# The reads of the mixture's gates, moved behind the first two ring steps of the next forward part

## The chip, the core and the metric

The kernel runs on one core of a Trainium2 chip. Its engines are TensorE (PE; PEld is its weight load), VectorE (DVE), ScalarE (ACT), GpSimd (POOL) and SyncE (SP). SP does no arithmetic here: it issues nearly all DMAs, in the order in which they are written. The metric is the device time of one execution in microseconds (us); lower is better.

## The reference

The input is a batch of 32 images. A tower of two layers turns each into 38 tokens of 192 features:

```
h = patches @ W + positions, behind two class tokens           # 32 x 38 x 192
h = h + state_space(layernorm(h))                              # 16 states per feature, a scan over 38 steps
h = h + two_of_eight_experts(layernorm(h))                     # 192 -> 768 -> 192 with gelu
h = h + up(ln(mamba_f(down)) + flip(ln(mamba_b(flip(down)))))  # a scan forward and one backward, 16 states
h = h + mixture(layernorm(h)): softmax over 8 scores, the best 2, each a 192 x 192 matrix
```

The last two lines matter here. Both scans compute, at each step t, `state = decay[t] * state + in[t]` for 192 features x 16 states. The mixture multiplies each token by the gates of its two chosen experts (the other six gates are zero) and puts the products through the eight matrices.

## The kernel before

**Groups and passes.** The batch is cut into 4 groups of 8 images (T = 304 tokens). A first pass does the first scan and the routing of all groups, then come the experts, whose last blocks overlap the start of the second pass. The second pass does the last two lines of the reference. It handles each group g in a forward part (`part_a`) and a backward part (`part_b`), of 12 ring steps each (`QSTEPS`). Software pipelining adds other groups' work: during group g's parts, the same engines do the output and gates of group g - 1 (`tail`), the front of group g + 1 (`nxt`) and, in the forward part, the mixture of group g - 2 (`mix`). So a mixture stands in the forward parts of groups 2 and 3, and two more behind the last scan.

**A ring step.** The scan runs over 16 states x 8 features on 128 partitions, two blocks of features at a time (128 x 608). Its inputs are rows of 304 values of step size and input, which DVE computes and SP writes to DRAM (`write_rows`: six DMAs, L621 to L623) and reads back, each row broadcast to 16 partitions (`fill_slot`, L510: one DMA of 304 KB into the ring `dA` and one into `BB`). `rows_there` makes SP wait until the six writes have landed. A ring of 4 slots holds the steps; `read_rows` waits until the scan four steps earlier has been done. Then for step c:
- ACT takes the exponential of `dA` in place (L956, two instructions). By its program it works two steps ahead of the others.
- DVE multiplies `BB` into PSUM (L1293) and scans (L1304) into one of two buffers `ST`.
- POOL multiplies the state by C into `PR` (L790). A scan waits for the product two steps before it.
- PE sums the product over states with four matmuls (`sum_step`).

**The gates of the mixture.** When group g - 1's gates are ready at the end of a backward part, SP writes them to DRAM (`write_gates`, L637), writes the next group's rows, and reads the gates back, broadcast over partitions, into the buffer `GX` (in the trace: `WX`): `read_gates`, one DMA of 1216 KB (L642) and two of 304 KB (L646). In the forward part that follows, POOL multiplies `GX` by the normalized tokens in six pieces, one behind each of the products 0 to 5 (`gate_inputs`, L798). Each piece waits for all three reads (`gates_in`). PE puts each piece through the experts' matrices (`mixture`, four matmuls a piece), at ring steps 1 to 6, behind `sum_step` 0 to 5. DVE adds the result at ring step 7 (`add_mixture`, L1549), and only then computes the rows of the backward part (`steps`, L1355 to L1364), for which SP waits.

**The order of the other engines around it.** On ACT, behind the exponential of step 4 come the square and copy of the other direction's output (L985, L986), a silu for the backward direction with a table load before and behind it (L909 to L917, L839), the exponentials of steps 5 to 7, and a copy of 24 rows (L921). PE's matmuls of the backward direction's step sizes (`project_steps`, `PS<-aP`) wait for L921. They stand in PE's order ahead of the last two pieces of the mixture. All orders are written out by hand in the functions; no scheduler changes them.

Of the kernel before, what the change touches and what calls it, by code (L numbers as in the profile page):

```python
# [7 lines left out]
GROUPS = 4  # L8
# [108 lines left out]
def vit_tower(nc, x_p, c128a, c64a, c128, c64, ex_m, ex_r, ex_b, out_m, out_r):  # L117
    fp32, bf16, i32, u32 = mybir.dt.float32, mybir.dt.bfloat16, mybir.dt.int32, mybir.dt.uint32
    ALU, ACT, AX = mybir.AluOpType, mybir.ActivationFunctionType, mybir.AxisListType
    with ExitStack() as ctx:  # L120
# [353 lines left out]
        def is_first(g):  # L474
            return isinstance(g, int) and g == 0
# [5 lines left out]
        def _(sp):  # L481
# [21 lines left out]
            def fill_slot(k, c, slot, signal):  # L503

                for kind, ring in enumerate((dAq, BBq)):
                    rows, per, j = rows_d[k, kind, 0:DM, :], MAIN_BLOCKS, c * QB
                    if j >= MAIN_BLOCKS:
                        rows, per, j = rows_d[k, kind, DM:D, :], REST_BLOCKS, j - MAIN_BLOCKS
                    rows = rows.rearrange("(i j) t -> i j t", j=per)[:, j:j + QB, :].rearrange("i j t -> i (j t)")
                    sp.dma_start(ring[:, slot].rearrange("p b t -> p (b t)"),  # L510
                                 rows.unsqueeze(0).broadcast_to([NS, FB, QB * T])).then_inc(signal.sem, 16)
# [90 lines left out]
            def load_next(g):  # L602
                sp.wait_ge(mixed.sem, mixed.after(g, TILES))
                load_keep(g + 1)
                sp.wait_ge(M.residual.sem, M.residual.after(g, 1))
                load_h(g + 1)

            def store(g):
                sp.wait_ge(final.sem, final.after(g, 1))
                sp.dma_start(out_m[bass.ds(g, 1), :, :].rearrange("g p t -> p (g t)"), Om[:, :]).then_inc(stored.sem, 16)  # L610
                sp.dma_start(out_r[bass.ds(g, 1), :, :].rearrange("g p t -> p (g t)"), Or[:, :]).then_inc(stored.sem, 16)

            def store_end(g):
                sp.wait_ge(stored.sem, stored.after(g, 32))
                sp.sem_inc(out_free.sem, 1)

            def write_rows(g, k):

                sp.wait_ge(Q.w_ready.sem, Q.w_ready.after(g, k + 1))
                for kind, x in enumerate((DIRS[k].DL, DIRS[k].WV)):  # L620
                    sp.dma_start(rows_d[k, kind, 0:DM, :], x[:, 0:T]).then_inc(rows_written.sem, 16)  # L621
                    sp.dma_start(rows_d[k, kind, DM:D, 0:HALF], x[0:DR, T:PK]).then_inc(rows_written.sem, 16)
                    sp.dma_start(rows_d[k, kind, DM:D, HALF:T], x[DR:128, T:PK]).then_inc(rows_written.sem, 16)  # L623

            def rows_there(g, k):
                sp.wait_ge(rows_written.sem, rows_written.after(g, 96 * (k + 1)))

            def read_rows(g, k, c):

                n, slot = k * QSTEPS + c, c % SLOTS  # L630
                if n >= SLOTS or not is_first(g):
                    sp.wait_ge(q_scanned.sem, q_scanned.after(g, n - SLOTS + 1))
                fill_slot(k, c, slot, landed[slot])

            def write_gates(g):
                sp.wait_ge(Q.gates_T_ready.sem, Q.gates_T_ready.after(g, 1))
                sp.dma_start(gates_d[:, :], Q.LW).then_inc(gates_out.sem, 16)  # L637

            def read_gates(g):

                sp.wait_ge(gates_out.sem, gates_out.after(g, 16))
                sp.dma_start(GX[:, 0:EXPERTS, :].rearrange("p e t -> p (e t)"),  # L642
                             gates_d.rearrange("e t -> (e t)").unsqueeze(0).broadcast_to([128, EXPERTS * T])).then_inc(gates_in.sem, 16)
                for h in range(2):
                    every = gates_d.rearrange("(e h) t -> h e t", h=2)[h:h + 1, :, :]
                    sp.dma_start(GX[h * DR:(h + 1) * DR, EXPERTS:, :], every.broadcast_to([DR, EXPERTS // 2, T])).then_inc(gates_in.sem, 16)  # L646
# [12 lines left out]
            for g in range(GROUPS):  # L659
                rows_there(g, 0)  # L660
                for c in range(QSTEPS):
                    read_rows(g, 0, c)
                write_rows(g, 1)
                rows_there(g, 1)
                for c in range(QSTEPS):
                    read_rows(g, 1, c)
                    if c == 4 and g + 2 < GROUPS:
                        load_next(g + 1)
                    if c == 8 and g >= 2:
                        store(g - 2)  # L670
                    if c == QSTEPS - 1 and g >= 2:
                        store_end(g - 2)
                if g:
                    write_gates(g - 1)
                if g + 1 < GROUPS:
                    write_rows(g + 1, 0)
                if g:
                    read_gates(g - 1)
            store(GROUPS - 2)
            store_end(GROUPS - 2)  # L680
            write_gates(GROUPS - 1)
# [1636 lines left out]
```

## Time and profile before

| what | us |
|---|---|
| timed runs | 966.21, 966.85, 961.38; median 966.21 |
| the profiled execution, its own time | 961.01 |
| its span, first to last instruction | 959.2 |
| PE busy | 741.7 (77%) |
| DVE busy | 564.3 (59%) |
| ACT busy | 403.8 (42%) |
| POOL busy | 395.1 (41%) |
| forward part of group 2, from the first scan's input to `add_mixture` | 716.5 to 742.4 |
| forward part of group 3, the same | 812.7 to 838.2 |

No engine is busy throughout: the kernel is a chain of stages in which the engines wait for one another, so the busy shares do not say which one a stage waits for.
### The profile page before, as it was taken

The page shows a single profiled execution, that of the slowest core. Times are in us where ns is not written, and L with a number is a line of the kernel's source. Part 1 is how long each engine was busy: PE and PEld are TensorE (multiplying, and loading weights), DVE is VectorE, ACT ScalarE, POOL GpSimd, SP SyncE. Part 2 cuts the span into 40 slices and gives each one's busy share as a digit, 9 for nine tenths or more (in the row PEclk, how much of TensorE's full clock was granted, in tenths as well). Part 3 has the DMA queues.
Part 4 walks back from the last instruction along what each step waited for, and adds up shares of the span by engine and source line. Part 5 has one row for each costly group of instructions (what it writes and reads, how often), then busy time and mean ns, then how long its engine had stood idle before and what let it go on. Part 6 is the DMA issues. An engine that isn't in the chain of part 4 may idle for free. (4 is left out here: it accounts for less than half of the span.)

```text
span 959.2 us, 11504 instructions
## 1 busy us (share of the span) xinstructions
PE 741.7 (77%) x3608; PEld 587.3 (61%) x3608; DVE 564.3 (59%) x968; ACT 403.8 (42%) x876; POOL 395.1 (41%) x311
## 2 busy tenths in 40 slices
PE   7877887784647879887999568797769986986756
PEld 5645656553437879787899346565556764663534
DVE  4167779679675613312112587888877787789320
ACT  1548374282225224322345356373617352733110
POOL 1045745665663321321003244653538333834503
PEclk8899999797667989999999789988978999897978
DMA  9469655355585567877676778697688657967211
GB/s 349 134 211 337 206 158 143 100 148 145 144 232 150 164 193 237 262 234 232 212 232 191 196 195 223 173 239 182 153 220 218 153 141 222 240 151 191 79 61 37
DMA packets 84668, 179.51 MB, mean 187 GB/s; under 512 B 12740, under 2 KB 32832, under 8 KB 83840
## 3 DMA queue, kind: packets, MB, share of 16 engines
q1 hardware_dynamic: 79776, 171.55, 63.3%
q0 software_dynamic: 4832, 7.24, 2.6%
q8 instruction: 28, 0.46, 0.2%
q14 instruction: 32, 0.26, 0.1%
HBM read 158.02 MB, written 20.69 MB: 186 GB/s over the span
## 5 line engine op out<-in xcount | busy, mean ns | idle before, releaser
L1670 PE MATMUL PS<-PR,CM 128*128 128x304 f32 (+1 forms) x672 | 186.3, 419 | 92.7 <-POOL PR L790 63.8
L790 POOL TENSOR_TENSOR PR<-ST,V 128x608 f32<-128x608 f32 x96 | 142.3, 1482 | 185.7 <-DVE ST L1304 155.5
L1670 PEld LDWEIGHTS PS<-PR,CM 128*128 128x128 f32 x672 | 126.5, 220 | 135.7 <-POOL PR L790 77.7
L956 ACT ACTIVATE dA<-dA,negA 128x304 f32<-128x304 f32 x192 | 93.6, 538 | 151.8 <-DMA BB<-rows_d 151.7
L1304 DVE TENSOR_TENSOR_SCAN ST<-dA,PS 128x608 f32<-128x608 f32 x96 | 136.3, 1420 | 15.1 <-ACT dA L956 10.9
L1008 ACT ACTIVATE HID<-PS,WX 128x128 f32<-128x128 f32 x204 | 59.5, 367 | 149.7 <-PE PS L1670 147.6
L703 POOL TENSOR_TENSOR dA<-dA,aP 128x607 f32<-128x607 f32 x48 | 70.7, 1475 | 73.1 <-ACT aP L976 71.2
L1293 DVE TENSOR_TENSOR PS<-BB,PS 128x608 f32<-128x608 f32 x96 | 76.2, 794 | 22.5 <-DMA BB<-rows_d 11.3
L1500 DVE TENSOR_TENSOR xp<-PS,WXB 128x192 f32<-128x192 f32 x34 | 12.2, 358 | 128.2 <-PE PS L1670 123.4
L1670 PE MATMUL PS<-XT,WX 128*128 128x128 f32 x408 | 84.1, 290 | 1.0 <-ACT HID L1008 1.0
L1670 PE MATMUL PS<-XT,WXR 128*128 128x128 f32 x408 | 83.8, 289 | 0.0
L718 POOL DMA_DIRECT2D outs_d<-xp x34 | 19.4, 570 | 148.0 <-DVE xp L1500 148.0
L1670 PE MATMUL PS<-WX,HID 128*128 128x192 f32 x408 | 74.1, 331 | 7.3 <-DVE XT L1493 6.1
L1670 PEld LDWEIGHTS PS<-WX,HID 128*128 128x128 f32 x408 | 67.5, 194 | 8.2 <-issue 6.1
L709 POOL TENSOR_TENSOR PR<-PR,ST 128x608 f32<-128x608 f32 x32 | 47.2, 1474 | 57.9 <-DVE ST L1283 57.7
L1283 DVE TENSOR_TENSOR_SCAN ST<-dA,PS 128x608 f32<-128x608 f32 x48 | 67.8, 1412 | 2.3 <-issue 1.3
L1670 PEld LDWEIGHTS PS<-XT,WX 128*128 128x128 f32 x408 | 67.0, 206 | 1.3 <-ACT HID L1008 1.3
L1670 PEld LDWEIGHTS PS<-XT,WXR 128*128 128x128 f32 x408 | 66.8, 206 | 0.0
L1670 PE MATMUL PS<-WX,CM 128*128 128x304 f32 x192 | 55.6, 431 | 11.0 <-POOL WX L798 10.6
L1670 PEld LDWEIGHTS PS<-WX,CM 128*128 128x128 f32 x192 | 37.1, 197 | 26.2 <-POOL WX L798 13.6
L1670 PE MATMUL PS<-HB,CM 96*128 96x152 f32 (+1 forms) x240 | 48.5, 353 | 0.2 <-ACT HB L1110 0.2
L1670 PEld LDWEIGHTS PS<-HB,CM 96*128 96x128 f32 x240 | 39.7, 202 | 8.0 <-issue 2.7
(363 smaller groups left out, 1287.8 us busy)
## 6 DMA issues: line engine op xcount, KB each, us to landing
dA<-rows_d SPq DMA_DIRECT2D x144, 304.0 KB
BB<-rows_d SPq DMA_DIRECT2D x144, 304.0 KB
WX<-ex_m SPq DMA_DIRECT2D x34, 576.0 KB
WX<-ex_m SPq DMA_DIRECT2D x34, 387.0 KB, 3.8
slots_d<-WXR SPq DMA_DIRECT2D x8, 960.0 KB, 8.2
WXR<-ex_r SPq DMA_DIRECT2D x34, 192.0 KB, 4.6
WX<-gates_d SPq DMA_DIRECT2D x4, 1216.0 KB, 6.3
CM<-c SPq DMA_DIRECT2D x1, 4430.0 KB, 19.6
```

What stands on the lines that cost most here:

```text
L703: nc.gpsimd.tensor_tensor(now[:, 1:], now[:, 1:], before[:, 0:QB * T - 1], ALU.mult).then_inc(ap_ready.sem, 1)
L709: nc.gpsimd.tensor_tensor(PR3[c % 3], PR3[c % 3], STq[:, c % 2], ALU.mult).then_inc(P.product.sem, 1)
L718: pool.dma_start(outs_d[b // HALF_BLOCKS][at:at + 128, :], YB[:, b % 3, :]).then_inc(out_rows[b % 3], 16)
L790: nc.gpsimd.tensor_tensor(PRq[:, c % 2], STq[:, c % 2], DIRS[k].Cw.unsqueeze(1).broadcast_to([128, QB, T]), ALU.mult).then_inc(q_product.s ...
L956: last = nc.scalar.activation(dAq[:, slot, i, :], dAq[:, slot, i, :], ACT.Exp, scale=negA[:, j:j + 1])
L1008: last = nc.scalar.activation(HX[:, p, f, :], PS[:, wide_bank(b, h), j * 128:(j + 1) * 128], ACT.Gelu, bias=WX[:, p, FFN + f:FFN + f + 1])
L1283: nc.vector.tensor_tensor_scan(flat(STq[:, c % 2], False), flat(dAq[:, slot], False), BP[0], 0.0, ALU.mult, ALU.add).then_inc(P.scanned.se ...
L1293: nc.vector.tensor_tensor(BPq[k], BBq[:, slot], BW[k].unsqueeze(1).broadcast_to([128, QB, T]), ALU.mult).then_inc(b_times_w.sem, 1)
L1304: nc.vector.tensor_tensor_scan(flat(STq[:, c % 2], back), flat(dAq[:, slot], back), BP[k][:, ::-1] if back else BP[k], 0.0, ALU.mult, ALU. ...
L1500: nc.vector.tensor_tensor(YB[:, p, :], PS[:, SHARED_BANK, 256:256 + D], WXB[:, p, :], ALU.add).then_inc(y_copied.sem, 1)
L1670: return nc.tensor.matmul(out, lhsT, rhs, start=first, stop=last)
```

## The change

`read_gates` of group g - 1 stood behind `write_rows` of group g + 1 and ahead of that group's `rows_there` and ring reads. Now it stands behind ring steps 0 and 1 of the forward part of group g + 1, and ahead of ring step 2. This concerns the gates of groups 0 and 1, read in the forward parts of groups 2 and 3. The gates of groups 2 and 3 are read behind the last scan, as before. Nothing is added or removed.

```
@@ second pass, SP @@
                 rows_there(g, 0)
                 for c in range(QSTEPS):
                     read_rows(g, 0, c)
+                    if c == 1 and g >= 2:
+                        read_gates(g - 2)
                 write_rows(g, 1)
...
                 if g + 1 < GROUPS:
                     write_rows(g + 1, 0)
-                if g:
-                    read_gates(g - 1)
+            read_gates(GROUPS - 2)
             store(GROUPS - 2)
```

Only SP's order changes. On SP at the start of group 2's forward part (`q_WV` is the last of the rows written, `dA` and `BB` are the ring, `WX` takes the gates; in brackets the semaphores that an instruction waits for), - is before and + is now:

```order
 L623 DMA rows_d<-q_WV 64x152
+L510 DMA dA<-rows_d 128x1x608 [waits q_scanned,rows_written]
+L510 DMA BB<-rows_d 128x1x608
+L510 DMA dA<-rows_d 128x1x608 [waits q_scanned]
+L510 DMA BB<-rows_d 128x1x608
 L642 DMA WX<-gates_d 128x2432 [waits gates_out]
 L646 DMA WX<-gates_d 64x4x304 x2
-L510 DMA dA<-rows_d 128x1x608 [waits q_scanned,rows_written]
-L510 DMA BB<-rows_d 128x1x608
-L510 DMA dA<-rows_d 128x1x608 [waits q_scanned]
-L510 DMA BB<-rows_d 128x1x608
```

The four ring reads of steps 0 and 1 have moved ahead of the three gate reads, and the wait for the written rows with them; the reads of step 2 follow the gates. The same piece stands once more, at the start of group 3's forward part.

On POOL, at the same place, the order is the same before and now (L790 are the products of steps 0 to 2, L798 the first pieces of the gates; the line numbers are those of before):

```order
L790 TENSOR_TENSOR PR<-ST,V 128x608 [waits q_summed,c_copied,q_scanned]
L798 TENSOR_TENSOR WX<-WX,q_Xm 128x608 [waits x_doubled,gates_in]
L790 TENSOR_TENSOR PR<-ST,V 128x608 [waits q_summed,q_scanned]
L798 TENSOR_TENSOR WX<-WX,q_Xm 128x608 [waits x_doubled,gates_in]
L790 TENSOR_TENSOR PR<-ST,V 128x608 [waits q_summed,q_scanned]
```

Nothing has moved here; the first L798 waits for `gates_in`, and the product of step 1 is queued behind it.

## Rows read from the trace of the kernel before

**Rows 1.** Chain of waits by time, groups 2 and 3: start us, us, engine
```profile
711.49 7.52 issue
...
720.58 21.35 PE PS L1670 x74
...
816.74 20.92 PE PS L1670 x74
```
**Rows 2.** Timeline of SP: start us, us, engine line op out<-in
```profile
701.45 0.60 SPq L623 DMA_DIRECT2D rows_d<-q_WV  x1
702.09 0.58 SPq L642 DMA_DIRECT2D WX<-gates_d  x1
704.23 0.73 SPq L510 DMA_DIRECT2D dA<-rows_d  x1
708.54 0.52 SPq L510 DMA_DIRECT2D dA<-rows_d  x1
...
800.49 0.60 SPq L623 DMA_DIRECT2D rows_d<-q_WV  x1
801.13 0.58 SPq L642 DMA_DIRECT2D WX<-gates_d  x1
```
**Rows 3.** Timeline of DVE; in brackets the idle time before and what ended it
```profile
716.53 0.80 DVE L1293 TENSOR_TENSOR PS<-BB,PS 128x608 f32<-128x608 f32 x1 [5.67 <-DMA BB<-rows_d]
741.95 0.47 DVE L1549 TENSOR_TENSOR Om<-q_Hm,PS 128x304 f32<-128x304 f32 x1 [2.27 <-PE PS L1670]
...
812.70 0.80 DVE L1293 TENSOR_TENSOR PS<-BB,PS 128x608 f32<-128x608 f32 x1 [5.60 <-DMA BB<-rows_d]
837.68 0.47 DVE L1549 TENSOR_TENSOR Om<-q_Hm,PS 128x304 f32<-128x304 f32 x1 [2.78 <-PE PS L1670]
```
**Rows 4.** Chain of waits by time, parts without gates: start us, us, engine
```profile
844.02 1.94 DMA rows_d<-p_WV
...
846.58 4.23 DMA BB<-rows_d
```
**Rows 5.** Busy us in stretches: PE, PEld, DVE, ACT, POOL, then PEclk, DMA share, GB/s
```profile
702.00:704.00 2.00, 2.00 (x14) 1.78 (x13) 2.00 (x3) 0.00 (x0) 1.11 (x2) 1.00 0.63 127
...
720.00:722.00 2.00, 1.42 (x3) 1.09 (x4) 1.98 (x3) 0.59 (x2) 2.00 (x3) 0.50 0.97 257
...
726.00:728.00 2.00, 2.00 (x9) 1.29 (x8) 1.86 (x3) 1.78 (x5) 1.69 (x2) 1.00 0.97 248
```
**Rows 6.** Timeline of ACT, groups 2 and 3
```profile
718.94 0.99 ACT L956 ACTIVATE dA<-dA,negA 128x304 f32<-128x304 f32 x2 [1.48 <-DMA BB<-rows_d]
...
726.20 0.99 ACT L956 ACTIVATE dA<-dA,negA 128x304 f32<-128x304 f32 x2 [1.40 <-DMA BB<-rows_d]
...
730.62 0.39 ACT L917 ACTIVATE p_Xm<-PS,CM 64x152 f32<-64x152 f32 x1
...
735.99 0.40 ACT L921 ACTIVATE aP<-PS 24x304 f32<-24x304 f32 x1
...
814.84 0.99 ACT L956 ACTIVATE dA<-dA,negA 128x304 f32<-128x304 f32 x2 [1.21 <-DMA BB<-rows_d]
...
831.20 0.40 ACT L921 ACTIVATE aP<-PS 24x304 f32<-24x304 f32 x1
```
**Rows 7.** Timeline of PE, groups 2 and 3
```profile
720.58 2.40 PE L1670 MATMUL PS<-PR,CM 128*128 128x304 f32 x4 [4.86 <-POOL PR L790]
...
725.74 1.19 PE L1670 MATMUL PS<-WX,CM 128*128 128x304 f32 x4
...
732.54 0.68 PE L1670 MATMUL PS<-p_UP,CM 128*128 128x304 f32 x2
...
737.65 1.19 PE L1670 MATMUL PS<-aP,CM 128*128 128x304 f32 x6
...
833.38 1.19 PE L1670 MATMUL PS<-aP,CM 128*128 128x304 f32 x6
```
**Rows 8.** Timeline of POOL, group 2
```profile
720.47 1.48 POOL L798 TENSOR_TENSOR WX<-WX,q_Xm 128x608 f32<-128x608 f32 x1
```

More of the change, by code:

```diff
@@ L662, in _ @@
                     read_rows(g, 0, c)
+                    if c == 1 and g >= 2:
+                        read_gates(g - 2)
                 write_rows(g, 1)
@@ L676, in _ @@
                     write_rows(g + 1, 0)
-                if g:
-                    read_gates(g - 1)
+            read_gates(GROUPS - 2)
             store(GROUPS - 2)
```

## The prediction

> **What bounds the kernel now.** I read the page, then the chain of waits, then the rows of each engine in the two stretches that the edit touches. These are the starts of the forward parts of groups 2 and 3, near 711 and 806 us. The chain [rows 1] shows 7.52 us of "issue" at 711.49, a wait whose cause it doesn't see, and then 74 matmuls in one unbroken run of 21.35 us (20.92 in group 3). DVE's rows say what the hole is: it stood idle for 5.67 us until step 0's BB had landed (716.53), and for 5.60 us in group 3 (812.70) [rows 3]. SP's rows say why: behind the last write of rows (701.45) it issued the gates (702.09), and the first ring read only at 704.23 [rows 2]. In a part without gates, step 0 landed at 846.58 + 4.23 = 850.81, 4.85 us behind the landing of the rows at 845.96 [rows 4].
>
> That invites the reading that two holes of 5.6 us go. I don't read it so. In the first stretch the DMA engines don't stop at step 0. ACT waits for every BB, to step 4 at 726.20 [rows 6], and the DMA share is 0.97 at 720 and at 726 [rows 5]. This transfer-bound stretch lasts from the gates to step 4, and the edit leaves its bytes the same and permutes them.
>
> **The change, part by part.**
>
> *The start of the transfers.* Before, the gates were issued at 702.09, while SP would have had to wait for the rows anyway. Now ring step 0 is first, and it needs the rows: 1.94 us from the last write's issue to its landing [rows 4], so 701.45 + 1.94 = 703.39. Everything then starts 703.39 - 702.09 = 1.30 us later. In group 3 it is 800.49 + 1.94 - 801.13 = 1.30 again [rows 2]. The DMA share at 702 to 704 was 0.63 [rows 5]: this is the stretch that the old order filled.
>
> *Steps 0 and 1* land early: step 0 at 703.39 + 4.85 = 708.2, before DVE is free at 716.53 - 5.67 = 710.86 [rows 3]. In group 3 it is 802.43 + 4.85 = 807.3 against 807.10. Both holes vanish from where they were.
>
> *The gates.* Gates, step 0 and step 1 are the same bytes in another order, so the last of the three lands where step 1 did, plus 1.30: 718.94 + 1.30 = 720.24, and 814.84 + 1.30 = 816.14 [rows 6]. POOL's first piece of the gates, which started at 720.47 [rows 8], can start at 720.24. POOL waits for it between the products of steps 0 and 1, and DVE's scan of step 3 waits for product 1. The stall has only moved from step 0 to step 2, which stands behind the gates in the queue.
>
> *Steps 2 to 4* land 1.30 later than before, step 4 at 727.50. The three issues of the gates end at about 703.39 + 2.5 + 2.1 = 708.0, ahead of step 2's 708.54 [rows 2], so SP delays none.
>
> *From step 4 to the mixture.* ACT worked without a hole from step 4's exponential (726.20) to L921, which ended at 735.99 + 0.40 = 736.39 [rows 6]. This 10.2 us follows step 4's landing, and now ends at 737.69. PE's matmuls on that copy started at 737.65 [rows 7]: PE came 1.26 us after ACT, because its run had begun late, at 720.58. Now PE is early and waits for ACT. Its first piece of the mixture can start at 720.24 + 1.48 = 721.72 instead of 725.74, and 6.80 us of work bring it to the backward projections, which need L917: 730.62 + 0.39 + 1.30 = 732.31. From there it takes 737.65 - 732.54 = 5.11 to 737.42, still ahead of 737.69. So these matmuls start at 737.69 instead of 737.65: **0.04 us lost**. In group 3, L921 ended at 831.60 and PE came at 833.38, 1.78 later [rows 6, 7]. Now 832.90: **0.48 us gained**. Behind them stand 4.30 us of matmuls in both groups, to the end of the mixture (741.95 and 837.68) [rows 3]. DVE gets there 2.27 and 2.78 us early, which covers its own 1.30.
>
> *The rest.* The rows of the backward part, its reads and PE's later matmuls follow that point and shift with it. The reads of groups 2 and 3 behind the last scan don't move.
>
> **Sum:** +0.04 - 0.48 = -0.44 us. The profiled execution took 961.01, so 960.6; it lies 5.20 below the median of the runs, so 966.21 - 0.44 = **965.8 us**, no change.
>
> *Bounds of the unknown.* No row shows gates behind ring steps. If ring steps 2 to 4 are not late at all, the gain is PE's lag, 1.26 + 1.78 = 3.04. On the other side, the same bytes, from the gates' issue to step 1's landing, took 718.94 - 702.09 = 16.85 us in group 2 and 814.84 - 801.13 = 13.71 in group 3, 3.14 apart. Both slow gives +2.66 in group 3, +2.7 in all; both quick gives -3.14 in group 2, -3.6 in all. I take the 1.30, which comes from the rows of this very wait.
>
> A rule speaks against the edit here. The Trainium skill, "DMA: Bandwidth & Descriptors", Rules for kernel authors, says to issue a transfer early and wait for it late, so that its fixed cost is covered. By that rule giving up the early issue costs the 1.30 twice; without it the sum would be -3.04 instead of -0.44. The share of 0.63 at 702 agrees.
>
> **The rivals.**
> 1. *The ring is not late* (0.12): the queue has room and steps 2 to 4 land as before. -3.04, 963.2 us. For it: 0.97 is not 1. Against: ACT's waits for each BB.
> 2. *The holes come back whole* (0.05): the queue never bound, PE runs on earlier, and keeps its clock. 5.67 + 5.60 = 11.27, and PE's first sum costs 1.19 instead of 2.40, twice: 2.42 more. 966.21 - 13.7 = 952.5. Against: it needs L921 5 us earlier too, and ACT cannot pass step 4's landing.
> 3. *Slower: the gates hold the ring longer* (0.17). Place: step 4's BB in front of ACT. It decides from a lateness of 1.26 us in group 2 and 1.78 in group 3; each us above is a us lost. At the bound of +2.7: 968.9. For it: group 2's slow transfers. Against: the bytes are the same.
> 4. *Slower: PE stays at the low clock* (0.03). At 720 to 722 the granted clock was 0.50, 1.2 GHz, behind PE's idle 4.86 us, and the four matmuls of a sum took 2.40; at 726 it was 1.00, 2.4 GHz, behind 5 us of unbroken matmuls, and four took 1.19 [rows 5, 7]. Now PE has a hole in front of the gates instead, and then works at POOL's pace. The 11.91 us from 725.74 to 737.65 would take 23.82: from 721.72 to 745.54, 7.9 us late, and in group 3 from 817.62 to 841.44, 8.1 late: 982.2. Against: at the low clock PE would be unbrokenly busy, and that is what brought the clock back. The Trainium skill, "TensorE: Matmul & The Clock Gate", Why this matters for your kernels, says that idle gaps between bursts return PE to half rate; the row at 720 agrees.
> 5. *The edit doesn't reorder the landings* (0.02): the 16 DMA engines serve gates and ring alike. 0 us, 966.2.
>
> **How the numbers follow.** The forecast has 0.61. The range goes from the fastest run less 3.6, 961.38 - 3.6 = 957.8, to the slowest plus 2.7, 966.85 + 2.7 = 969.6: **957.5 to 970**, which leaves out rivals 2 and 4 and some of the runs' own spread. A change under 1% (9.7 us) cannot be told here, since three runs spread over 5.5 us. Faster by more: rival 2, 0.05. Slower by more: rival 4 and a little of 3, 0.04. The same: 0.91.
>
> **What would show it.** In the changed profile, DVE's idle time in front of step 0 is under 1 us in both groups and one of 3 to 5 us stands in front of step 2. POOL's first L798 starts near 720 and 816, behind a wait for the gates. ACT still waits for each BB to step 4, about 1.3 later. PE waits for ACT in front of `PS<-aP`, and L1549 stands within 1 us of 741.95. It would be wrong if L1549 came 4 us earlier (rival 2) or later (rivals 3, 4).

## The result, and the profile after

The changed kernel is slower, by 0.65%: 969.75 us (median of 14 runs, 967.4 to 979.37) against 963.25 of the kernel before in the same job (14 runs), ratio 1.0065, 95% interval 1.0040 to 1.0090. A second job gave 1.0096 (1.0067 to 1.0126). The forecast was no change: 966.21 - 0.44 = 965.77. Of the 3.98 us between that and 969.75, the change took +6.50 instead of -0.44, and the kernel before was 2.96 faster in this job than the median the forecast started from (6.50 + 0.44 - 2.96 = 3.98). The profiled execution took 968.73 us, its span is 966.0. Ratios, here and below, leave out the few executions of a kernel that took over 1.5% longer than its fastest, in a slower state.

In the rows below the lines of the code have moved by one or two (the DVE multiply is L1294, `add_mixture` L1550, POOL's gates L799, the squares L986 and L987).

SP did what the edit says. Timeline of SP after, group 2: start us, us, line, output and input.

```profile
700.22 0.60 SPq L623 DMA_DIRECT2D rows_d<-q_WV  x1
702.18 0.55 SPq L510 DMA_DIRECT2D dA<-rows_d  x1
...
705.45 0.59 SPq L642 DMA_DIRECT2D WX<-gates_d  x1
...
707.40 1.10 SPq L510 DMA_DIRECT2D dA<-rows_d  x1
```

The first ring read is issued 1.96 us behind the last write of rows; before, the gates stood 0.64 behind it [rows 2]. Both holes of DVE have moved from step 0 to step 2, as forecast. Timeline of DVE after, groups 2 and 3; in brackets the idle time before, and what ended it.

```profile
720.80 0.80 DVE L1294 TENSOR_TENSOR PS<-BB,PS 128x608 f32<-128x608 f32 x1 [5.53 <-DMA BB<-rows_d]
...
744.00 0.47 DVE L1550 TENSOR_TENSOR Om<-q_Hm,PS 128x304 f32<-128x304 f32 x1 [4.83 <-PE PS L1671]
...
821.21 0.80 DVE L1294 TENSOR_TENSOR PS<-BB,PS 128x608 f32<-128x608 f32 x1 [6.35 <-DMA BB<-rows_d]
...
843.00 0.47 DVE L1550 TENSOR_TENSOR Om<-q_Hm,PS 128x304 f32<-128x304 f32 x1 [4.83 <-PE PS L1671]
```

In front of L1550 DVE now waits 4.83 us for PE, where it waited 2.27 and 2.78 [rows 3]: PE is late there, and DVE is not. The start of such a stretch, counted from the start of the span, differs between executions by up to 9 us with nothing changed ahead of it, so I measure it from the last write of rows (issue of L623) to the start of `add_mixture`. Before: 741.95 - 701.45 = 40.50 and 837.68 - 800.49 = 37.19, together 77.69 [rows 2, 3]. After: 744.00 - 700.22 = 43.78 and 843.00 - 801.56 = 41.44, together 85.22. These 7.53 us are about the loss: the spans of the two profiled executions differ by 6.8, the medians by 6.50.

Where they come from stands on PE. Timeline of PE after, groups 2 and 3; `p_OM,ones_bn` is the matmul that takes the variance of the backward direction's output of the group before (the old direction), over squares that ACT computes.

```profile
720.08 1.29 PE L1671 MATMUL PS<-WX,CM 128*128 128x304 f32 x4 [2.98 <-POOL WX L799]
721.51 1.29 PE L1671 MATMUL PS<-PR,CM 128*128 128x304 f32 x4
727.32 1.33 PE L1671 MATMUL PS<-p_OM,ones_bn 96*96 96x304 f32 x2 [4.52 <-ACT q_Cm L987]
728.44 2.23 PE L1671 MATMUL PS<-WX,CM 128*128 128x304 f32 x4
730.46 2.23 PE L1671 MATMUL PS<-PR,CM 128*128 128x304 f32 x4
732.49 1.23 PE L1671 MATMUL PS<-WX,CM 128*128 128x304 f32 x4
...
739.70 1.19 PE L1671 MATMUL PS<-aP,CM 128*128 128x304 f32 x6
...
819.59 1.29 PE L1671 MATMUL PS<-WX,CM 128*128 128x304 f32 x4 [2.91 <-POOL WX L799]
821.02 2.15 PE L1671 MATMUL PS<-PR,CM 128*128 128x304 f32 x4
826.33 1.33 PE L1671 MATMUL PS<-p_OM,ones_bn 96*96 96x304 f32 x2 [3.15 <-ACT q_Cm L987]
827.45 2.23 PE L1671 MATMUL PS<-WX,CM 128*128 128x304 f32 x4
829.48 2.22 PE L1671 MATMUL PS<-PR,CM 128*128 128x304 f32 x4
```

The first piece of the mixture ran at 720.08, early, as forecast. Then PE stood idle for 4.52 us in front of the variance (3.15 in group 3), and the groups of four matmuls behind it took 2.23 us instead of 1.19. In group 3 the clock had fallen earlier: the sum at 821.02 already took 2.15 us, behind the 2.91 us in which PE waited for the gates. The squares that PE waited for at the variance stand on ACT behind step 4's exponential. Timeline of ACT after, group 2.

```profile
720.80 0.99 ACT L957 ACTIVATE dA<-dA,negA 128x304 f32<-128x304 f32 x2 [8.20 <-DMA BB<-rows_d]
...
725.66 0.99 ACT L957 ACTIVATE dA<-dA,negA 128x304 f32<-128x304 f32 x2 [1.44 <-DMA BB<-rows_d]
726.56 0.40 ACT L986 ACTIVATE p_OM<-PS 96x304 f32<-96x304 f32 x1
726.86 0.40 ACT L987 ACTIVATE q_Cm<-PS 96x304 f32<-96x304 f32 x1
...
735.80 0.41 ACT L922 ACTIVATE aP<-PS 24x304 f32<-24x304 f32 x1 [0.26 <-PE PS L1671]
```

PE's output, on which the squares are taken, had long been there (PE was idle), but ACT stood in front of step 4's exponential, which waits for its BB. The last row shows the path that I had forecast: ACT's copy of 24 rows (L921 before) now waits for PE, and not PE for it.

The kernel before had the same two operations, and they met almost exactly. Timeline of PE before, groups 2 and 3:

```profile
727.85 0.75 PE L1670 MATMUL PS<-p_OM,ones_bn 96*96 96x304 f32 x2
...
823.66 0.68 PE L1670 MATMUL PS<-p_OM,ones_bn 96*96 96x304 f32 x2
```

Timeline of ACT before, groups 2 and 3. This is the copy behind the square; PE waits for both, and the copy ends 0.05 and 0.65 us ahead of PE:

```profile
727.40 0.40 ACT L986 ACTIVATE q_Cm<-PS 96x304 f32<-96x304 f32 x1
...
822.60 0.41 ACT L986 ACTIVATE q_Cm<-PS 96x304 f32<-96x304 f32 x1
```

PE's late run had brought it there just when the squares were done, at full clock. The stretch splits at the variance:

| from | to | before, groups 2 and 3 | after, groups 2 and 3 | difference |
|---|---|---|---|---|
| last write of rows | variance | 26.40, 23.17 | 27.10, 24.77 | +0.70, +1.60 |
| variance | `add_mixture` | 14.10, 14.02 | 16.68, 16.67 | +2.58, +2.65 |

The lateness of the variance, which the wait causes, costs 2.30 us in all. The slower matmuls behind it, of equal number and order, cost 5.23. A second profiled execution of the same kernel (e7 below) gives 1.40 and 5.27. The granted clock says the same. Stretches of 2 us after: busy us of PE, PEld, DVE, ACT, POOL with instructions, then granted clock, DMA share, GB/s.

```profile
722.00:724.00 2.00, 0.80 (x4) 0.25 (x2) 1.90 (x2) 0.77 (x2) 1.51 (x2) 1.00 1.05 258
724.00:726.00 2.00, 0.00 (x0) 0.00 (x0) 1.78 (x3) 0.56 (x2) 2.00 (x2) 0.93 1.03 254
726.00:728.00 2.00, 0.69 (x2) 0.46 (x3) 1.89 (x2) 1.98 (x5) 2.00 (x3) 0.50 1.05 260
...
730.00:732.00 2.00, 2.00 (x6) 1.32 (x5) 0.00 (x0) 1.96 (x4) 0.00 (x0) 0.50 1.03 259
732.00:734.00 2.00, 2.00 (x8) 1.50 (x7) 1.15 (x1) 1.94 (x5) 1.16 (x1) 0.86 0.30 91
```

In group 2 it fell to 0.50 (1.2 GHz) in PE's idle time, stayed there through the variance and the next two groups of four, and came back in the stretch from 732. Before, at 726 to 728, it was 1.00 [rows 5].

### The profile page after: what moved, and what is told of

The parts are those of the page before. It is cut to its first block and busy times, and to the rows that moved or that the text cites. A ratio compares the mean times of both kernels' runs of the same rounds, so it can differ in the third digit from the quotient of the medians.

```text
span 966.0 us, 11504 instructions
## 1 busy us (share of the span) xinstructions
PE 740.8 (77%) x3608; PEld 583.0 (60%) x3608; DVE 564.7 (58%) x968; ACT 403.7 (42%) x876; POOL 394.9 (41%) x311
## 5 line engine op out<-in xcount | busy, mean ns | idle before, releaser
L1671 PE MATMUL PS<-PR,CM 128*128 128x304 f32 (+1 forms) x672 | 183.9, 414 | 82.6 <-POOL PR L791 53.1
L1671 PEld LDWEIGHTS PS<-PR,CM 128*128 128x128 f32 x672 | 124.4, 217 | 125.7 <-POOL PR L791 67.6
L1294 DVE TENSOR_TENSOR PS<-BB,PS 128x608 f32<-128x608 f32 x96 | 76.2, 793 | 23.8 <-DMA BB<-rows_d 12.7
L1671 PE MATMUL PS<-WX,CM 128*128 128x304 f32 x192 | 60.2, 456 | 17.3 <-POOL WX L799 16.9
L1671 PEld LDWEIGHTS PS<-WX,CM 128*128 128x128 f32 x192 | 39.1, 209 | 35.9 <-POOL WX L799 22.4
```

The source lines that it names most:

```text
L1294: nc.vector.tensor_tensor(BPq[k], BBq[:, slot], BW[k].unsqueeze(1).broadcast_to([128, QB, T]), ALU.mult).then_inc(b_times_w.sem, 1)
L1671: return nc.tensor.matmul(out, lhsT, rhs, start=first, stop=last)
```

## The experiments

**Theory A**: PE, in order, waits in front of the variance for ACT's squares, which stand behind step 4's exponential, and works at half clock behind the wait. **Theory B**: the ring's lateness costs, by way of ACT's copy of 24 rows. **Theory C**: the later gates themselves cost. All kernels were timed in 5 rounds beside the kernel before, 6 to 12 runs of each. The stretch runs, as above, from the last write of rows to `add_mixture`, in one profiled execution of each. What such an execution does outside the two stretches differs by several us (e1's span is 7.6 us longer than that of before, with stretches 1.3 shorter), so the stretches say where time goes, and the ratios what it is worth.

| kernel | stretch, groups 2 and 3 | sum against before | ratio (95%) |
|---|---|---|---|
| changed | 43.78, 41.44 | +7.5 | 1.0065 (1.0040 to 1.0090) |
| e7, changed again | 42.80, 41.56 | +6.7 | 1.0096 (1.0067 to 1.0126) |
| e1, squares ahead of step 2's exponential | 37.71, 38.69 | -1.3 | 1.0013 (0.9980 to 1.0046) |
| e2, matmuls that keep the clock | 38.96, 40.47 | +1.7 | 1.0008 (0.9969 to 1.0047) |
| e3, squares ahead of step 4's exponential | 37.42, 38.42 | -1.9 | 1.0014 (0.9978 to 1.0049) |
| e4, silus and squares in ACT's hole | 37.32, 36.51 | -3.9 | 0.9990 (0.9957 to 1.0023) |
| e5, before, squares behind the silus | 44.47, 40.77 | +7.5 | 1.0091 (1.0059 to 1.0124) |
| e6, before, ACT's order of e4 | 42.41, 41.30 | +6.0 | 1.0060 (1.0034 to 1.0087) |
| e8, e4, gates behind step 0 | 42.69, 46.53 | +11.5 | 1.0106 (1.0076 to 1.0135) |
| e9, before, squares as in e3 | 38.62, 36.91 | -2.2 | 1.0017 (0.9990 to 1.0043) |
| e10, e4 and projections in front | 37.68, 34.92 | -5.1 | 0.9967 (0.9933 to 1.0001) |
| e11, e2 and e3 together | 39.59, 38.52 | +0.4 | 1.0015 (0.9990 to 1.0039) |
| e12, e10 again | 36.24, 35.35 | -6.1 | 0.9950 (0.9923 to 0.9977) |

**e1 and e3: the squares earlier.** On the changed kernel, in the forward parts with a mixture:

```
+                early = None not in (g, tail, mix)
                 for n in range(QSTEPS):
+                    if early and n == 0:        # e3: n == 2
+                        output(tail, 1)
                     if g is not None:
                         decay_ahead(g, 0, n + AHEAD)
                     if n == 2:
-                        if tail is not None:
+                        if tail is not None and not early:
                             output(tail, 1)
```

> The changed kernel, with one move on ACT in the two forward parts that have a mixture: the square and copy of the other direction's output stand ahead of the exponential of ring step 2 instead of behind that of step 4. Theory A (PE waits for these squares in front of the variance matmul, 4.5 and 3.2 us, and then works at the low clock): the hole goes, add_mixture comes some 4 us earlier in both groups, in all 8 us below the changed kernel, a ratio to before of about 0.998. Theory B (the loss is that ring steps 2 to 4 land later, by way of ACT's copy of 24 rows): at most 1 us comes back, ratio 1.005 to 1.006. Theory C (POOL's wait for the gates, 5.0 and 5.7 us, holds the products): nothing comes back, 1.006.

> The changed kernel with a smaller move of the squares on ACT: they stand between the exponentials of steps 3 and 4, one landing (2.4 us in group 2, 1.6 in group 3) earlier than in the changed kernel. Theory A: the hole in front of the variance matmul shrinks from 4.5 and 3.2 us to about 2, add_mixture 2.4 and 1.6 us earlier, and up to 2.7 each more if the clock then holds: 4 to 9 us below the changed kernel, ratio to before 0.997 to 1.002. Theories B (ring late) and C (gates late): 1.006.

No transfer was moved, and the loss went: 1.0013 and 1.0014, with intervals that end at 1.0046 and 1.0049. B and C, by which 1.005 to 1.006 had to stay, fall as the main cause. The stretches became 8.8 and 9.4 us shorter than the changed kernel's, the medians against the kernel before only by some 5; A's 0.998 for e1 was too good by 0.3% and lies at the edge of the interval. In e1 PE no longer waited at the variance. In e3 the wait was not gone but shorter. Timeline of PE of e3, groups 2 and 3.

```profile
730.82 0.75 PE L1674 MATMUL PS<-p_OM,ones_bn 96*96 96x304 f32 x2 [2.27 <-ACT q_Cm L987]
731.41 1.19 PE L1674 MATMUL PS<-WX,CM 128*128 128x304 f32 x4
...
820.57 1.29 PE L1674 MATMUL PS<-WX,CM 128*128 128x304 f32 x4 [3.07 <-POOL WX L799]
822.00 2.29 PE L1674 MATMUL PS<-PR,CM 128*128 128x304 f32 x4
825.73 1.33 PE L1674 MATMUL PS<-p_OM,ones_bn 96*96 96x304 f32 x2 [1.44 <-ACT q_Cm L987]
826.85 2.23 PE L1674 MATMUL PS<-WX,CM 128*128 128x304 f32 x4
```

In group 2 the 2.27 us left the clock up. In group 3 it had already fallen behind the wait for the gates (2.29 at 822.00), and stayed down, as in the changed kernel. So a part of C holds, by way of the clock: in e1's group 3 a wait of 4.01 us for the gates alone, with none at the variance, left the sum behind it at 2.40 us and the variance at 1.22.

**e2: the wait stays, the clock is kept.** Matmuls that add zero fill PE's two holes, in front of the first piece of the mixture and in front of the variance:

```
+                            if None not in (g, mix):
+                                for _ in range(12):
+                                    mm(PS[0:DR, Q_BANK, 0:128], cm("end"), ones_d[:, :], False, False)
                             direction_var(tail, 1)
...
+                    for _ in range(10 if g < 2 else 0):
+                        mm(PS[0:DR, Q_BANK, 0:128], cm("end"), ones_d[:, :], False, False)
```

> The changed kernel, with matmuls that add zeros to the mixture's open sum while PE waits: 10 ahead of the mixture's first piece and 12 ahead of the variance matmul, in the two forward parts that have a mixture. All waits stay. Theory A with a clock term: the variance, one piece and one sum cost 0.75 + 1.19 + 1.19 instead of 1.33 + 2.23 + 2.23, 2.7 us less per group, so some 5 us below the changed kernel, ratio to before about 1.001. If PE's low clock is covered by other waits, and by theories B (ring late) and C (gates late): 1.006 as the changed kernel.

Timeline of PE of e2, group 2; `ones_d,CM` are the twelve fillers.

```profile
726.30 2.83 PE L1671 MATMUL PS<-ones_d,CM 128*64 128x128 f32 x24
729.76 0.75 PE L1671 MATMUL PS<-p_OM,ones_bn 96*96 96x304 f32 x2 [0.63 <-ACT q_Cm L987]
730.35 1.19 PE L1671 MATMUL PS<-WX,CM 128*128 128x304 f32 x4
```

PE still waits for the squares, but comes out at 1.19 us per four. From the variance to `add_mixture` it took 14.10 us in both groups, as before (14.10 and 14.02) and not 16.68 and 16.67: 5.15 us came back, near the 5.23 that the split puts down to the clock. Ahead of the variance e2 was 2.23 us quicker than the changed kernel in group 2 and 1.60 slower in group 3, so that the stretches gave back 5.8 of the 7.5 in all, 4.8 and 1.0; the ratio is 1.0008. So in the changed kernel most of the loss is the clock. Since the fillers stand in both holes, e2 does not tell what each hole does to the clock.

**e5: the loss without moving a byte.** On the kernel before, the squares trade places with the silus behind them:

```
                     if n == 2:
-                        if tail is not None:
+                        if tail is not None and not late:
                             output(tail, 1)
                         if g is not None:
...
                             inputs(g, 1)
+                            if late:
+                                output(tail, 1)
```

> The kernel before, gates ahead of the ring as ever; only ACT's squares of the old direction now stand behind its four silus instead of ahead of them (groups 2 and 3). Theory A (what costs is TensorE's wait for these squares, in order, and the half clock behind it): the squares end near 731.1 instead of 727.8, so TensorE waits some 3.2 us in front of the variance and then runs part of the mixture at 1.20 clock; the stretch from the last write of rows to the end of the mixture becomes 4 to 6 us longer in each group, ratio 1.008 to 1.012. The loss then appears without any gates moved. Theory B (what costs is the ring that lands late, by way of ACT's copy of 24 rows) and theory C (what costs are the gates that land late): no transfer is moved and the copy keeps its place, so 1.000, within 0.002.

Ratio 1.0091, as A said; B and C said 1.000. The stretches are 3.97 and 3.58 us longer, a little under A's 4 to 6. Timeline of PE of e5, groups 2 and 3.

```profile
727.39 1.19 PE L1673 MATMUL PS<-PR,CM 128*128 128x304 f32 x4
732.20 1.05 PE L1673 MATMUL PS<-p_OM,ones_bn 96*96 96x304 f32 x2 [3.62 <-ACT q_Cm L986]
733.03 2.23 PE L1673 MATMUL PS<-WX,CM 128*128 128x304 f32 x4
735.06 1.62 PE L1673 MATMUL PS<-PR,CM 128*128 128x304 f32 x4
736.52 1.19 PE L1673 MATMUL PS<-WX,CM 128*128 128x304 f32 x4
...
832.22 0.75 PE L1673 MATMUL PS<-p_OM,ones_bn 96*96 96x304 f32 x2 [2.37 <-ACT q_Cm L986]
```

The same wait, with the gates in their old place, and in group 2 slow matmuls behind it. In group 3 the clock stayed up behind 2.37 us (0.75 for the variance). Split at the variance, the lateness costs 2.29 and 3.50 us here and the clock 1.68 and 0.08: the wait makes the loss in both kernels, but how much of it comes by the clock differs.

**e9: the repair where nothing is broken.** The edit of e3 on the kernel before.

> The kernel before with the one edit on ACT that was worth 0.5 to 0.8% on the changed kernel: the squares ahead of step 4's exponential. Theory A: before, TensorE came to the variance at 727.85 when the squares had just ended (727.80), out of an unbroken run at full clock; there is no wait to take away and no clock to keep. Ratio 1.000, within 0.002. Rival (the earlier squares are worth something by themselves, and the runs on the changed kernel showed only that): 0.992 to 0.995.

1.0017 (0.9990 to 1.0043): no gain, as A said. PE came to the variance of group 2 at 728.29 without a wait. The earlier squares pay only where PE waits for them.

**e11: both repairs.** The edits of e2 and e3 together.

> The changed kernel with both repairs: squares ahead of step 4's exponential, and matmuls that add zero in TensorE's two holes, so that the clock stays up. Theory A (wait and clock add up): about 37 us from the last write of rows to the end of the mixture in both groups, ratio 0.997 to 1.000. If the two repairs give back the same loss, or the fillers cost as much as they keep: 1.001 as each of them alone. Theory B (the ring's lateness): 1.005.

1.0015, the second case: once the squares are early, the fillers cost at least what they keep; in the profiled execution the stretches are 2.3 us longer than e3's. In group 2 the variance then stood directly behind the fillers, at 734.55, and waited for nothing else.

**e4, e6, e8: ACT's hole.** With the gates behind step 1, ACT waits 8.20 us in front of step 2's exponential. e4 puts silus, squares and the load of the table behind them there:

```
+                    if early and n == 0:
+                        act.wait_ge(y_gated.sem, y_gated.after(tail, 2))
+                        inputs(g, 1)
+                        output(tail, 1)
+                        ln_and_exp()
                     if g is not None:
                         decay_ahead(g, 0, n + AHEAD)
...
-                        if g is not None:
+                        if g is not None and not early:
```

> The changed kernel, with all of ACT's work that needs no ring step put into its idle 8 us between the exponentials of steps 1 and 2 in the two forward parts that have a mixture: the silu of the backward direction with its table load, the squares, and the table load back. Theory A: as with the squares alone, and the exponential of step 5 follows its landing (728.1) instead of 731.8, so add_mixture comes some 5 us earlier in both groups: ratio to before about 0.996. Theory B (ring late): the copy of 24 rows comes some 3 us earlier per group, ratio about 1.000. Theory C (gates late): 1.006.

e6 has this order on the kernel before, and e8 has it with the gates behind step 0 (`if c == 0 and g >= 2` in place of `c == 1`).

> The kernel before, gates ahead of the ring, with ACT's silus and squares put ahead of step 2's exponential as in the run that had both in ACT's hole. It crosses that run: same order on ACT, the gates' reads at the old place. Theory A: with the gates ahead of the ring TensorE didn't wait at the variance, so there is nothing to win there, and ACT has no hole at this place: its squares wait for TensorE's output near 725, so step 2's exponential comes some 5 us late. Ratio 1.000 to 1.006; this order pays only with the gates behind the ring. Rival (the order on ACT is better by itself and the gates' place is worth nothing): 0.999 as with the gates behind the ring, within 0.002.

> The changed kernel with ACT's silus and squares ahead of step 2's exponential, and the gates' reads behind ring step 0 instead of behind step 1. Theory A: the gates land some 2.2 us earlier and step 1 later by their 2.1 us; TensorE's first piece of the mixture comes near 721 instead of 723.3, the variance waits for nothing, the stretch to the end of the mixture is 0 to 2 us shorter than with the gates behind step 1: ratio 0.996 to 0.999. Theory B (the ring is what costs): step 1 is late instead of step 2, the same stretch, 0.999 to 1.001. Theory C (the gates are what costs): 2 us less in each group, 0.995.

e4 gave 0.9990: the loss is gone. Its stretches are 6.5 and 4.9 us shorter than the changed kernel's, as A said, but the ratio lies nearer to B's 1.000 than to A's 0.996, so e4 does not decide between them. e6 gave 1.0060, the upper end of what A said, and the rival's 0.999 falls: with the gates in front ACT's long hole stands ahead of step 0, its silus waited for DVE until 725.76, and the exponentials of steps 2 to 5 ran only from 730.15. e8 was a miss of mine: 1.0106 where I had expected a gain. Its rows show why. Timeline of DVE of e8, group 2; `p_WV<-PS,aP` is the first piece of the gating that makes the old direction's output.

```profile
723.24 0.80 DVE L1300 TENSOR_TENSOR PS<-BB,PS 128x608 f32<-128x608 f32 x1 [5.50 <-DMA BB<-rows_d]
...
725.65 0.45 DVE L1377 TENSOR_TENSOR p_WV<-PS,aP 128x304 f32<-128x304 f32 x1
...
732.20 1.42 DVE L1311 TENSOR_TENSOR_SCAN ST<-dA,PS 128x608 f32<-128x608 f32 x1 [4.72 <-issue]
```

Timeline of ACT of e8, the same stretch:

```profile
726.68 0.55 ACT L910 ACTIVATE aP<-PS 128x456 f32<-128x456 f32 x1 [1.15 <-DVE HID L1379]
...
731.12 3.62 ACT L957 ACTIVATE dA<-dA,negA 128x304 f32<-128x304 f32 x8
```

The gating stands on DVE behind step 1's scan, and step 1 is now the step that lands behind the gates. ACT's silus and squares wait for the gating, and the exponentials of steps 2 to 5 wait behind them. It is the same kind of error as in the prediction: I looked at when the data land, not at what stands in each engine's order behind the instruction that waits. By the order of the program, the place behind step 1 is the earliest behind the ring's start that leaves the gating alone. The gates behind step 0 with ACT's old order were not run.

**e7: the changed kernel again**, in the job of e5, e6 and e8.

> The changed kernel as it is, beside the others of this job. If the first comparison held: ratio 1.0065, within 0.003. If it was chance: 1.000 to 1.003.

1.0096, a little above the range that I had given, and clear of 1.003: the first result was no chance.

**e10 and e12: a version that beats both.** On e4, PE's first eight matmuls of the backward projections, which stood behind the fourth piece of the mixture, go into the idle time in front of the first:

```
                     if g is not None:
-                        if n == 4:
+                        if n == (4 if tail is None or mix is None else 1):
                             project_states(g, 1)
...
-                        if n == 5:
+                        if n == (4 if early else 5):
                             projected(g, 1)
```

> The changed kernel with ACT's silus and squares in front of step 2's exponential (ratio 0.999 in its run), and besides TensorE's first eight matmuls of the backward projections, 2.05 us, moved from behind the fourth piece of the mixture into TensorE's idle 2.3 us in front of the first; the copy of 24 rows follows one step earlier. Theory A (what is left of the stretch is TensorE's work behind its last wait): 2.05 us less in each group, and in group 3 the clock is back sooner (up to 1 us): 4 to 6 us, ratio 0.993 to 0.996. Rival (POOL's alternating pieces, 1.43 us each from the gates' landing on, end last): 0.998 to 1.000.

> The kernel with silus, squares and the first backward projections in front, once more, since its first interval (0.9933 to 1.0001) just touches no change. If it beats the kernel before, as its two stretches say (37.68 and 34.92 us against 40.51 and 37.19): 0.995 to 0.998 again, and the two intervals together lie below 1. If the first result was chance: 0.999 to 1.001.

0.9967 (0.9933 to 1.0001), and 0.9950 (0.9923 to 0.9977) in the second job: together it beats the kernel before by a third to half a per cent. Against e4 the stretches of e10 are 1.2 us shorter in all, those of e12 2.2, of the 4.10 us of matmuls that moved. Timeline of PE of e10, group 2.

```profile
718.92 0.78 PE L1677 MATMUL PS<-p_UP,CM 128*128 128x304 f32 x2 [0.65 <-ACT p_Xm L918]
...
722.31 1.29 PE L1677 MATMUL PS<-WX,CM 128*128 128x304 f32 x4 [0.57 <-POOL WX L799]
...
727.39 1.29 PE L1677 MATMUL PS<-PR,CM 128*128 128x304 f32 x4 [0.81 <-POOL PR L791]
728.82 1.29 PE L1677 MATMUL PS<-WX,CM 128*128 128x304 f32 x4
730.25 1.29 PE L1677 MATMUL PS<-PR,CM 128*128 128x304 f32 x4
```

Here the groups of four follow one another at POOL's pace, 1.43 us, instead of PE's own 1.02: the rival of that run holds in part. Of the kernels run, the moved gates pay only where ACT's and PE's orders are changed to suit them. The earlier projections on the kernel before, without the gates moved, were not run; e6 shows only that ACT's part of the change costs there.

## Why the prediction was wrong

*The start of the transfers, 1.30 us later.* Right in kind: the step behind the gates whose landing counts, step 4, came 25.44 us behind the last write of rows (725.66) where it had been 24.75 (726.20) [rows 2, 6], 0.69 later. In group 3 ACT started it 23.11 us behind (824.67) and before 20.91 (821.40), 2.20 later. The mean is 1.45. The two groups differ by the tail of the landings. In the traces a step's two reads land in 32 parts together. The first 30 of step 4 were in by 724.13 and 821.26 before, and by 724.83 and 822.99 after: 1.93 and 0.66 us later behind the write, 1.30 in the mean, as in the sum. The last part came 2.04 and 0.12 us behind these before, and 0.81 and 1.66 after.

*The holes only move.* Right in kind: none in front of step 0 in group 2 and 0.27 us in group 3, and 5.53 and 6.35 us in front of step 2 (I had said 3 to 5).

*The gates.* Right, or a little better: POOL's first piece started 18.34 us behind the last write of rows (718.56), where it had been 19.02 [rows 8]; the sum had 720.24 - 701.45 = 18.79.

*From step 4 to the mixture.* This is **the step that failed**: "Its first piece of the mixture can start at 721.72 instead of 725.74, and 6.80 us of work bring it to the backward projections". I took these 6.80 us from PE's unbroken run before, and laid them 4 us earlier. But the run holds the variance, which waits for ACT's squares, and those stand behind step 4's exponential: a wait that I had put at nothing. In the rows of before no wait is seen there, since PE came 0.05 us after the squares (0.65 in group 3). Less this slack, step 4's lateness gives 0.64 and 1.55 us, and the variance came 0.70 and 1.60 later. PE came 4.43 and 3.09 us earlier behind the write to its first piece, where I had 4.02, and could not use it: the run breaks behind its first two groups of four. The terms +0.04 and -0.48 became 0.70 + 2.58 = +3.28 and 1.60 + 2.65 = +4.25. e1 and e3 take the loss away with the transfers as they are, and e5 makes it with no gates moved. The Trainium skill, "TensorE: Matmul & The Clock Gate", Step-by-step: what each phase is for, says that matmuls stay in program order and that only weight loads are pulled ahead; the trace agrees, no matmul passed the variance in 4.52 us.

*The end of the path.* So PE did not wait for L921. The copy waited 0.26 us for PE, and `PS<-aP` came at 739.70. With this wait in the sum, and the clock up, the -0.44 would have been +2.30; the clock makes it 7.53.

*The clock.* Rival 4 had the right mechanism at 0.03, with the wrong size and, in group 2, the wrong place: the whole stretch of 11.91 us at half clock, 16 us in both groups. I held against it that PE would be unbrokenly busy. It was not: it was idle in front of the variance, and the half clock then lasted only for the variance and two groups of four (in group 3 also for the sum ahead of them, behind the wait for the gates, the place that rival 4 named). It cost 5.23, of which e2 gave back 5.15. I had looked for PE's idle time at the head of the run alone.

*Rival 3* named the right place on ACT, step 4's BB, and too high a threshold: lateness was to cost from 1.26 and 1.78 us on, and it cost from 0.05 and 0.65 on, the slack of the squares.

*The baseline.* The 966.21 was 2.96 above the 14 runs' median, and the range had been widened by the spread of three runs. That 969.75 still lies inside it, by 0.25, is luck. A small slip changes nothing: with both groups quick, group 2 gives 0.04 - 3.14 = -3.10.

Open: why the last part of a step's reads trails by 2.04 us in one stretch and by 0.12 in another; no experiment looked at it. Open too is how much of the 2.65 us in group 3 belongs to the wait for the gates, behind which the clock fell, and how much to the wait at the variance. And the profiles of e1, e3 and e9 show stretches 1 to 2 us shorter than before, while their ratios are 1.0013 to 1.0017. The intervals of e1 and e3 allow both, that of e9 (from 0.9990) does not: its execution was as long as that of before (span 959.1 against 959.2), so it lost elsewhere what its stretches gained.

## What to carry to other kernels

When an engine's run is to start earlier, go through every wait inside the run: one that showed no idle time before may have been met with no slack, because the run was late. Where such a wait then appears on PE, price the clock behind it too; here that was 5.23 us to 2.30 of lateness, and in e5 1.76 to 5.79. And here moving a transfer paid only when the orders of the engines around the old hole and the new one were changed with it.

## What the runs showed of the hardware

Of the 32 parts in which a step's reads land, the last trailed the first 30 by 2.04 us in one stretch and by 0.12 in another (step 4 before, groups 2 and 3), and ACT started the step 0.03 and 0.02 us behind it.
